# Chunk 1's inputs and head weights asked for on the SP queue, and the bias made later, in a gated low-rank kernel

## The chip, the core and the metric

One core of a Trainium2 chip. The metric is the time of the kernel on the device in microseconds (us), the median over runs. The core has TensorE (PE, matmuls, with its weight loads shown apart as PEld), VectorE (DVE), ScalarE (ACT), GpSimd (POOL) and SyncE (SP); SP and ACT each issue transfers on a queue of their own, and 16 DMA engines carry them all.

## The reference

For 2048 tokens of width 512: a linear layer, plus for each token the two best of 8 experts by logits (with 5.0 added for the expert that the sequence's id names), each expert a rank-16 update, and the input added back.

```python
x = x + L0(x, ids, W, Wr, A, B)     # x: (64, 32, 512)

def L0(x, ids, W, Wr, A, B):        # W 512x512, Wr 8x512, A 8x16x512, B 8x512x16
    base = einsum('btd,od->bto', x, W)
    logits = einsum('btd,ed->bte', x, Wr) + one_hot(ids, 8)[:, None, :] * 5.0
    topw, topi = top_k(logits, 2)
    gates = sum(one_hot(topi, 8) * softmax(topw)[..., None], axis=-2)
    h = einsum('btd,erd->bter', x, A)
    lora_out = einsum('bter,bte,eor->bto', h, gates, B)
    return base + 2.0 * lora_out
```

## The kernel before

The tokens form 16 tiles of 128. The contraction over 512 is cut into 4 chunks of 128 (k = 0 to 3). The stationary operand is a tile's x, transposed; the moving operand is the row of weights of that chunk, 648 columns: 392 *heads* columns (256 columns of W, the 128 of A and the 8 of Wr, names `heads_cols`, `heads_ps`) and 256 *base* columns (the rest of W, `base_cols`, `base_ps`).

To keep float32 accuracy, x and the weights are each split in an upper part (rounded to fp32r) and a lower part (the difference), and each product is made three times: upper by upper, upper by lower, lower by upper (n = 0, 1, 2). The parts are made on the core: `x_hi` by ACT (`chunk_upper`, L234), `x_lo` by POOL (`chunk_lower`, L213), the upper weights `w_hi` by ACT (`w_upper`, L237) but for the heads columns of chunks 0 and 1, which DVE makes (`heads_upper`, L369), and the lower weights `w_lo` by DVE (`w_lower`, L365).

Each engine runs its own program, written out by hand, and all order between engines comes from semaphores. There is no scheduler. The program starts with tiles 0 and 1 together, chunk by chunk, as the data arrives. `first_sb` holds for each chunk the x of these two tiles (256 columns), 4 columns with the ids, and the 648 weight columns. Its transfers are these: SP issues x and ids of chunk 0 (L166, 130 KB), the base weights of chunk 0 (L167, 128 KB), the base weights of chunk 1 (L168, 128 KB), and chunks 2 and 3 whole (L170, 454 KB each), then x of tile 2, b, and the groups of three tiles. ACT issues the head weights of chunk 0 (L255, 196 KB) and x, ids and head weights of chunk 1 (L256, 326 KB).

PE first runs seven matmuls on constants (L509), then one product of chunk 0 straight from float32 (L514), which needs only x and the head weights of chunk 0, and then the split products (all of them at L436). For chunk 1 it takes in this order: upper heads, upper base, the products with `x_lo`, then those with `w_lo` heads and `w_lo` base. Chunks 2 and 3 follow in nearly the same order. After that come tile 2 and a steady loop over the other tiles.

DVE starts with chunk 0 (`heads_upper(0)`, `w_lower` for heads and base), then makes the bias (L379: 5.0 where the expert's number equals the id, from `expert`, which POOL makes, and the ids in chunk 0's transfer), then chunk 1 (`heads_upper(1)` at L382, which waits for `chunk_landed[0]`, then `w_lower` for heads and base), then chunks 2 and 3, b, and from there the choice of experts. The bias is first read at L307, when PE has finished the heads of tile 0.

Of the kernel before, what the change touches and what calls it, by code (L numbers as in the profile page):

```python
# [23 lines left out]
HEADS = REST + ER + E  # L24
# [14 lines left out]
def cond_resid_program(nc: bass.Bass, first: bass.AP, xT: bass.AP, x: bass.AP,  # L39
# [11 lines left out]
    with ctx:  # L51
# [103 lines left out]
        @block.sync  # L155
        def _(sp):
            def load(dst, src, t, n, landed):
                sp.dma_start(dst[:, bass.ds(t, n), :], src[:, bass.ds(t, n), :]).then_inc(landed, 16)

            def store(t, n):  # L160
                sp.dma_start(out[:, bass.ds(t, n), :], out_sb[:, bass.ds(t, n), :]).then_inc(out_stored, 16)

            def load_xT(t, n, landed):
                load(xT_sb, xT, t - len(FIRST), n, landed)

            sp.dma_start(first_sb[:, 0, 0:FIRST_X + IDS], first[:, 0, 0:FIRST_X + IDS]).then_inc(x_landed, 16)  # L166
            sp.dma_start(w_sb[:, 0, base_cols], w[:, 0, base_cols]).then_inc(wb_landed, 16)  # L167
            sp.dma_start(w_sb[:, 1, base_cols], w[:, 1, base_cols]).then_inc(wb1_landed, 16)  # L168
            for k in range(2, KC):
                sp.dma_start(first_sb[:, k, :], first[:, k, :]).then_inc(chunk_landed[k - 1], 16)  # L170
            load_xT(2, 1, xT_third)
            sp.dma_start(b_sb[:, :], b).then_inc(b_landed, 16)

            load_xT(3, SLOTS, xT_group)
            load(x_sb, x, 0, SLOTS, x_group)
            with sp.Fori(0, GROUPS - 2) as g:
                sp.wait_ge(xT_group, 16 * g + 16)
                sp.wait_ge(x_group, 16 * g + 16)
                load_xT(SLOTS * g + 3 + SLOTS, SLOTS, xT_group)
                load(x_sb, x, SLOTS * g + SLOTS, SLOTS, x_group)  # L180
            sp.wait_ge(x_group, 16 * (GROUPS - 1))
            load(x_sb, x, GROUPED - SLOTS, SLOTS, x_group)
            load_xT(GROUPED, TILES - GROUPED, xT_last)
            load(x_sb, x, GROUPED, TILES - GROUPED, x_last)
            with sp.Fori(0, GROUPS) as g:
                sp.wait_ge(out_made, SLOTS * g + SLOTS)
                store(SLOTS * g, SLOTS)
            for t in range(GROUPED, TILES - 2):
                sp.wait_ge(out_made, t + 1)
                store(t, 1)  # L190

            for t in range(TILES - 2, TILES):
                sp.wait_ge(heads_read, t + 1)
                sp.dma_start(out[:, t, BASE:O], out_sb[:, t, BASE:O]).then_inc(out_stored, 16)
                sp.wait_ge(out_made, t + 1)
                sp.dma_start(out[:, t, 0:BASE], out_sb[:, t, 0:BASE]).then_inc(out_stored, 16)
            sp.wait_ge(out_stored, 16 * (GROUPS + TILES - 2 - GROUPED + 4))
# [33 lines left out]
        @block.scalar  # L231
        def _(act):
            def chunk_upper(k):
                nc.scalar.activation(x_hi[:, 0:2, chunks[k]], first_x[k], ACT.Copy).then_inc(chunk_hi_made, 1)  # L234

            def w_upper(k, cols):
                nc.scalar.activation(w_hi[:, k, cols], w_sb[:, k, cols], ACT.Copy).then_inc(w_hi_made, 1)  # L237

            def x_upper(t, s, landed, count):

                act.wait_ge(landed, count)
                if not (isinstance(t, int) and t < SLOTS):
                    act.wait_ge(base_done, t - SLOTS + 1)
                nc.scalar.activation(x_hi[:, s, :], xT_sb[:, t - len(FIRST), :], ACT.Copy).then_inc(x_hi_made, 1)  # L244

            def ghT_upper(t, s, src=ghT_ps):
                act.wait_ge(transposed, t + 1)
                nc.scalar.activation(ghT_hi[s][:, :], src[:, 0:P], ACT.Copy).then_inc(ghT_hi_made, 1)  # L248

            def exponential(t):  # L250
                act.wait_ge(top_made, t + 1)
                nc.scalar.activation(e2[:, :], top[:, 0:1], ACT.Exp, scale=-1.0,  # L252
                                     bias=top[:, 1:2]).then_inc(e2_made, 1)

            act.dma_start(w_sb[:, 0, heads_cols], w[:, 0, heads_cols]).then_inc(wh_landed, 16)  # L255
            act.dma_start(first_sb[:, 1, 0:FIRST_X + IDS + HEADS],  # L256
                          first[:, 1, 0:FIRST_X + IDS + HEADS]).then_inc(chunk_landed[0], 16)
            act.wait_ge(x_landed, 16)
            chunk_upper(0)
            act.wait_ge(wb_landed, 16)  # L260
            w_upper(0, base_cols)
            for k in range(1, KC):
                act.wait_ge(chunk_landed[k - 1], 16)
                chunk_upper(k)
                if k == 1:
                    act.wait_ge(wb1_landed, 16)
                    w_upper(k, base_cols)
                else:
                    w_upper(k, all_cols)
            x_upper(2, 2, xT_third, 16)  # L270
            act.wait_ge(b_landed, 16)
            nc.scalar.activation(b_hi[:, :], b_sb[:, :], ACT.Copy).then_inc(b_hi_made, 1)
            exponential(0)

            def step(t, j, landed, count):

                x_upper(t + 1, (j + 1) % SLOTS, landed, count)
                ghT_upper(t - 1, (j - 1) % SLOTS)
                exponential(t)

            exponential(1)
            ghT_upper(0, 0)
            with act.Fori(0, GROUPS - 1) as g:
                for j in range(2, 2 + SLOTS):
                    step(SLOTS * g + j, j, xT_group, 16 * g + 16)
            for t in range(GROUPED - 1, TILES - 1):
                step(t, t, xT_last, 16)
            last = TILES - 1
            act.wait_ge(x_last, 16)
            act.wait_ge(out_made, last - SLOTS + 1)  # L290
            nc.scalar.activation(base_ps[last % SLOTS][:, 0:BASE], x_sb[:, last, 0:BASE],
                                 ACT.Copy).then_inc(last_x_placed, 1)
            exponential(last)
            ghT_upper(last - 1, (last - 1) % SLOTS)
            ghT_upper(last, last % SLOTS, warm_ps)

        @block.vector
        def _(dve):
# [69 lines left out]
            def heads_upper(k):  # L368
# [5 lines left out]
            w_lower(0, heads_cols)  # L374
            dve.wait_ge(w_hi_made, 1)
            w_lower(0, base_cols)
            dve.wait_ge(expert_made, 1)
            dve.wait_ge(x_landed, 16)
            nc.vector.tensor_scalar(bias[:, :], expert[:, :], ids_sb, LANG_BIAS, ALU.is_equal,  # L379
                                    ALU.mult).then_inc(bias_made, 1)  # L380
            dve.wait_ge(chunk_landed[0], 16)
            heads_upper(1)  # L382
            dve.wait_ge(wh_hi_made, 2)
            w_lower(1, heads_cols)
            dve.wait_ge(w_hi_made, 2)
            w_lower(1, base_cols)
            for k in range(2, KC):
# [249 lines left out]
```

## Time and profile before

| | us |
|---|---|
| median of 3 runs | 79.89 |
| lowest and highest | 79.57, 80.69 |
| the profiled execution | 79.78 |
| its span | 78.0 |
| PE busy in it | 74.6 (96%) |
| PE weight loads (PEld) | 70.8 (91%) |
| DVE busy | 48.5 (62%) |
| ACT busy | 22.4 (29%) |
| POOL busy | 22.4 (29%) |

The span is what the trace covers; the time of an execution has a little more around it. A busy share is an average over the whole span. PE is busy almost throughout, so that the profile has to be read at the places where it could have been held up, above all while the first data arrives.

### The profile page before, as it was taken

What the parts mean: (1) busy time and instruction counts of PE and PEld (TensorE: products, weight loads), DVE (VectorE), ACT (ScalarE), POOL (GpSimd) and SP (SyncE); (2) the same over time, 40 slices, a digit from 0 to 9 for tenths busy, and PEclk for the clock granted to TensorE, in tenths of its full rate; (3) what the DMA queues carried; (4) which work ended last, traced back from release to release, by engine and by line L of the source; (5) the groups of instructions that cost most, each with busy time, mean ns of one, the idle gap of its engine ahead of it and who ended that gap; (6) DMA issues with size and microseconds to landing.
All of it is one profiled execution on the core that took longest, in us unless ns stands there. A gap on an engine that the chain in (4) does not pass through costs nothing.

```text
span 78.0 us, 1627 instructions
## 1 busy us (share of the span) xinstructions
PE 74.6 (96%) x502; PEld 70.8 (91%) x502; DVE 48.5 (62%) x220; ACT 22.4 (29%) x57; POOL 22.4 (29%) x26
## 2 busy tenths in 40 slices
PE   5999999999999999999999999999999999999960
PEld 2269999899999999999999999999999999999950
DVE  0097587878864828283755829283755739787750
ACT  1743941514502314140504113140404023122100
POOL 4053725064160514124060605123060606000000
PEclk9999999999999999999999999999999999999999
DMA  1999994499389389999920000350000072032143
GB/s 13 317 312 358 424 413 192 50 384 380 48 303 429 60 274 420 437 248 377 415 95 0 0 0 0 167 236 0 0 0 0 0 296 107 0 134 97 42 139 135
DMA packets 4037, 14.24 MB, mean 183 GB/s; under 512 B 448, under 2 KB 1472, under 8 KB 3776
## 3 DMA queue, kind: packets, MB, share of 16 engines
q1 hardware_dynamic: 3744, 13.65, 47.8%
q10 hardware_dynamic: 288, 0.53, 1.9%
q8 instruction: 2, 0.03, 0.2%
q14 instruction: 3, 0.02, 0.1%
HBM read 9.99 MB, written 4.19 MB: 182 GB/s over the span
## 4 chain that ended last, share of the span: by engine, by line
PE 96%; DVE 1%; issue 0%
PE heads_ps L436 43%; PE base_ps L436 28%; PE heads_ps L476 5%; PE base_ps L476 5%; PE warm_ps L509 4%; PE base_ps L480 2%; PE heads_ps L480 2%; PE ghT_ps L467 2%; PE heads_ps L514 2%; PE base_ps L460 2%; DVE out_sb L428 1%; PE warm_ps L467 0%
## 5 line engine op out<-in xcount | busy, mean ns | idle before, releaser
L209 POOL TENSOR_TENSOR x_lo<-xT_sb,x_hi 128x512 fp32r<-128x512 f32 x14 | 18.1, 1294 | 38.2 <-ACT x_hi L244 36.8
L436 PE MATMUL heads_ps<-w_hi,x_hi 128*128 128x392 f32 x63 | 22.7, 368 | 0.0
L436 PE MATMUL heads_ps<-w_lo,x_hi 128*128 128x392 f32 x63 | 20.9, 340 | 0.0
L436 PE MATMUL heads_ps<-w_hi,x_lo 128*128 128x392 f32 x63 | 20.8, 342 | 0.0
L436 PE MATMUL base_ps<-w_hi,x_lo 128*128 128x256 f32 x60 | 16.6, 283 | 0.0
L436 PE MATMUL base_ps<-w_hi,x_hi 128*128 128x256 f32 x60 | 16.6, 288 | 0.0
L436 PE MATMUL base_ps<-w_lo,x_hi 128*128 128x256 f32 x60 | 16.3, 280 | 0.0
L301 DVE TENSOR_TENSOR ghT_lo<-ghT_ps,ghT_hi 128x128 fp32r<-128x128 f32 x15 | 4.4, 291 | 14.8 <-ACT ghT_hi L248 14.7
L248 ACT ACTIVATE ghT_hi<-ghT_ps 128x128 fp32r<-128x128 f32 x15 | 4.1, 275 | 29.5 <-PE ghT_ps L467 29.5
L436 PEld LDWEIGHTS heads_ps<-w_hi,x_hi 128*128 128x128 f32 x63 | 11.8, 190 | 0.8 <-issue 0.3
L436 PEld LDWEIGHTS base_ps<-w_hi,x_hi 128*128 128x128 f32 x60 | 11.5, 193 | 0.4 <-ACT w_hi L237 0.3
L436 PEld LDWEIGHTS heads_ps<-w_lo,x_hi 128*128 128x128 f32 x63 | 11.7, 189 | 0.0
L436 PEld LDWEIGHTS heads_ps<-w_hi,x_lo 128*128 128x128 f32 x63 | 11.6, 188 | 0.0
L436 PEld LDWEIGHTS base_ps<-w_hi,x_lo 128*128 128x128 f32 x60 | 11.4, 192 | 0.0
L436 PEld LDWEIGHTS base_ps<-w_lo,x_hi 128*128 128x128 f32 x60 | 11.3, 189 | 0.0
L252 ACT ACTIVATE e<-top 128x1 f32<-128x1 f32 x16 | 4.7, 296 | 15.2 <-DVE top L312 15.2
L244 ACT ACTIVATE x_hi<-xT_sb 128x512 fp32r (+1 forms) x14 | 8.7, 621 | 0.4 <-issue 0.4
L346 DVE TENSOR_TENSOR out_sb<-heads_ps,x_sb 128x256 f32 (+1 forms) x16 | 6.7, 419 | 1.1 <-PE heads_ps L480 1.1
L336 DVE SCALAR_TENSOR_TENSOR gh<-heads_ps,rden,gate 128x128 f32<-128x128 f32 x16 | 5.6, 351 | 1.7
L351 DVE TENSOR_TENSOR out_sb<-base_ps,x_sb 128x256 f32 (+1 forms) x15 | 6.2, 415 | 0.0
L365 DVE TENSOR_TENSOR w_lo<-first_sb,w_hi 128x392 fp32r<-128x392 f32 (+1 forms) x8 | 4.5, 596 | 1.5 <-ACT w_hi L237 1.4
L213 POOL TENSOR_TENSOR x_lo<-first_sb,x_hi 128x256 fp32r<-128x256 f32 (+1 forms) x5 | 3.5, 705 | 5.1 <-ACT x_hi L234 5.1
(53 smaller groups left out, 99.9 us busy)
## 6 DMA issues: line engine op xcount, KB each, us to landing
x_sb<-in_x SPq DMA_DIRECT2D x4, 768.0 KB, 5.5
out<-out_sb SPq DMA_DIRECT2D x4, 768.0 KB, 4.3
xT_sb<-in_xT SPq DMA_DIRECT2D x3, 768.0 KB, 4.2
xT_sb<-in_xT SPq DMA_DIRECT2D x1, 1024.0 KB, 6.4
x_sb<-in_x SPq DMA_DIRECT2D x1, 1024.0 KB, 9.4
first_sb<-in_first SPq DMA_DIRECT2D x2, 454.0 KB, 5.6
out<-out_sb SPq DMA_DIRECT2D x2, 256.0 KB, 2.1
out<-out_sb SPq DMA_DIRECT2D x4, 128.0 KB, 1.8
```

Source lines behind the costliest of these rows:

```text
L209: nc.gpsimd.tensor_tensor(x_lo[:, s, :], xT_sb[:, t - len(FIRST), :], x_hi[:, s, :].bitcast(FP32), ALU.subtract).then_inc(x_lo_made, 1)
L213: nc.gpsimd.tensor_tensor(x_lo[:, tiles, chunks[k]], first_x[k][:, tiles, :], x_hi[:, tiles, chunks[k]].bitcast(FP32), ALU.subtract).then_ ...
L244: nc.scalar.activation(x_hi[:, s, :], xT_sb[:, t - len(FIRST), :], ACT.Copy).then_inc(x_hi_made, 1)
L248: nc.scalar.activation(ghT_hi[s][:, :], src[:, 0:P], ACT.Copy).then_inc(ghT_hi_made, 1)
L252: nc.scalar.activation(e2[:, :], top[:, 0:1], ACT.Exp, scale=-1.0, bias=top[:, 1:2]).then_inc(e2_made, 1)
L301: nc.vector.tensor_tensor(ghT_lo[s][:, :], src[:, 0:P], ghT_hi[s][:, :].bitcast(FP32), ALU.subtract).then_inc(ghT_lo_made, 1)
L336: nc.vector.scalar_tensor_tensor(gh[s][:, :].rearrange("p (e r) -> p e r", r=R), heads_ps[s][:, REST:REST + ER].rearrange("p (e r) -> p e ...
L346: nc.vector.tensor_tensor(out_sb[:, t, BASE:O], heads_ps[s][:, 0:REST], x_sb[:, t, BASE:O], ALU.add).then_inc(heads_read, 1)
L351: nc.vector.tensor_tensor(out_sb[:, t, 0:BASE], base_ps[s][:, 0:BASE], x_sb[:, t, 0:BASE], ALU.add).then_inc(out_made, 1)
L365: nc.vector.tensor_tensor(w_lo[:, k, cols], w_sb[:, k, cols], w_hi[:, k, cols].bitcast(FP32), ALU.subtract).then_inc(w_lo_made, 1)
L436: return nc.tensor.matmul(dst, xs[:, s, chunks[k]], ws[:, k, cols], start=(k == 0 and n == 0), stop=(k == KC - 1 and n == last_n))
L476: nc.tensor.matmul(dst, ghT_hi[s][:, :], bs[:, cols], start=False, stop=False, skip_group_check=True)
```

## The change

The transfer of chunk 1 (x, ids and head weights, 326 KB) is no longer issued by ACT behind the head weights of chunk 0. SP issues it, third in its queue: behind the base weights of chunk 0 and ahead of the base weights of chunk 1. On DVE the upper and lower head weights of chunk 1 are made before the bias, and the lower base weights of chunk 1 after it. Nothing else differs, and PE's program is the same row for row.

```diff
--- before.py
+++ after.py
@@ -165,6 +165,8 @@
 
             sp.dma_start(first_sb[:, 0, 0:FIRST_X + IDS], first[:, 0, 0:FIRST_X + IDS]).then_inc(x_landed, 16)
             sp.dma_start(w_sb[:, 0, base_cols], w[:, 0, base_cols]).then_inc(wb_landed, 16)
+            sp.dma_start(first_sb[:, 1, 0:FIRST_X + IDS + HEADS],
+                         first[:, 1, 0:FIRST_X + IDS + HEADS]).then_inc(chunk_landed[0], 16)
             sp.dma_start(w_sb[:, 1, base_cols], w[:, 1, base_cols]).then_inc(wb1_landed, 16)
             for k in range(2, KC):
                 sp.dma_start(first_sb[:, k, :], first[:, k, :]).then_inc(chunk_landed[k - 1], 16)
@@ -253,8 +255,6 @@
                                      bias=top[:, 1:2]).then_inc(e2_made, 1)
 
             act.dma_start(w_sb[:, 0, heads_cols], w[:, 0, heads_cols]).then_inc(wh_landed, 16)
-            act.dma_start(first_sb[:, 1, 0:FIRST_X + IDS + HEADS],
-                          first[:, 1, 0:FIRST_X + IDS + HEADS]).then_inc(chunk_landed[0], 16)
             act.wait_ge(x_landed, 16)
             chunk_upper(0)
             act.wait_ge(wb_landed, 16)
@@ -374,14 +374,14 @@
             w_lower(0, heads_cols)
             dve.wait_ge(w_hi_made, 1)
             w_lower(0, base_cols)
+            dve.wait_ge(chunk_landed[0], 16)
+            heads_upper(1)
+            dve.wait_ge(wh_hi_made, 2)
+            w_lower(1, heads_cols)
             dve.wait_ge(expert_made, 1)
             dve.wait_ge(x_landed, 16)
             nc.vector.tensor_scalar(bias[:, :], expert[:, :], ids_sb, LANG_BIAS, ALU.is_equal,
                                     ALU.mult).then_inc(bias_made, 1)
-            dve.wait_ge(chunk_landed[0], 16)
-            heads_upper(1)
-            dve.wait_ge(wh_hi_made, 2)
-            w_lower(1, heads_cols)
             dve.wait_ge(w_hi_made, 2)
             w_lower(1, base_cols)
             for k in range(2, KC):
```

SP's program at its start, before the change (`first_sb` is the tile that holds the first chunks; 128x260 is x and ids of chunk 0, 128x256 base weights, 128x908 a whole chunk):

```order
L166 DMA first_sb<-in_first 128x260
L167 DMA first_sb<-in_first 128x256
L168 DMA first_sb<-in_first 128x256
L170 DMA first_sb<-in_first 128x908 x2
L158 DMA xT_sb<-in_xT 128x512
L172 DMA b_sb<-in_b 128x512
```

and after it:

```order
L166 DMA first_sb<-in_first 128x260
L167 DMA first_sb<-in_first 128x256
L168 DMA first_sb<-in_first 128x652
L170 DMA first_sb<-in_first 128x256
L172 DMA first_sb<-in_first 128x908 x2
L158 DMA xT_sb<-in_xT 128x512
L174 DMA b_sb<-in_b 128x512
```

The row of 128x652 (chunk 1's x, ids and head weights) is new, and every row below it stands one place further back.

DVE's program, the piece that differs, with the semaphores that each row waits for (the rows of w_lo are lower weights, 128x392 heads and 128x256 base; the CAST of w_hi makes chunk 1's upper head weights):

```order
 L365 TENSOR_TENSOR w_lo<-first_sb,w_hi 128x392 [waits wh_hi_made]
 L365 TENSOR_TENSOR w_lo<-first_sb,w_hi 128x256 [waits w_hi_made]
-L379 TENSOR_SCALAR bias<-expert,first_sb 128x8 [waits x_landed,expert_made]
 L369 CAST w_hi<-first_sb 128x392 [waits chunk_landed1]
 L365 TENSOR_TENSOR w_lo<-first_sb,w_hi 128x392 [waits wh_hi_made]
+L383 TENSOR_SCALAR bias<-expert,first_sb 128x8 [waits x_landed,expert_made]
 L365 TENSOR_TENSOR w_lo<-first_sb,w_hi 128x256 [waits w_hi_made]
 L365 TENSOR_TENSOR w_lo<-first_sb,w_hi 128x392 [waits w_hi_made]
```

The bias has moved down by two rows, past chunk 1's upper and lower head weights.

## Rows read from the trace of the kernel before

**Rows 1.** The page: its span, and the chain that ended last by engine.
```profile
span 78.0 us, 1627 instructions
...
PE 96%; DVE 1%; issue 0%
```

**Rows 2.** Chain in order of time: start us, us, what.
```profile
0.78 3.14 PE warm_ps L509 x7
3.93 1.58 PE heads_ps L514 x2
...
5.83 0.72 PE base_ps L436 x4
6.55 0.35 PE heads_ps L436 x2
```

**Rows 3.** Timeline, DVE: start us, us, engine line, operation, tiles, [idle before <-releaser].
```profile
3.75 0.37 DVE L369 CAST w_hi<-first_sb 128x392 fp32r<-128x392 f32 x1 [3.75 <-DMA first_sb<-in_first]
4.15 1.45 DVE L365 TENSOR_TENSOR w_lo<-first_sb,w_hi 128x392 fp32r<-128x392 f32 x2
5.52 0.49 DVE L379 TENSOR_SCALAR bias<-expert,first_sb 128x8 f32<-128x8 int32 x1
5.92 0.35 DVE L369 CAST w_hi<-first_sb 128x392 fp32r<-128x392 f32 x1
6.31 1.04 DVE L365 TENSOR_TENSOR w_lo<-first_sb,w_hi 128x392 fp32r<-128x392 f32 x2
```

**Rows 4.** Busy us of PE, PEld, DVE, ACT, POOL; PEclk, DMA share, GB/s.
```profile
3.86:6.26 2.40, 2.40 (x7) 1.77 (x7) 2.37 (x5) 1.24 (x4) 1.46 (x3) 1.00 1.00 321
6.26:11.96 5.70, 5.70 (x40) 5.70 (x39) 3.79 (x9) 3.15 (x6) 2.52 (x4) 1.00 1.03 405
```

**Rows 5.** Timeline, PE's weight loads (PEld).
```profile
5.30 0.66 PEld L436 LDWEIGHTS base_ps<-w_hi,x_hi 128*128 128x128 f32 x2 [0.32 <-ACT w_hi L237]
...
6.87 0.30 PEld L436 LDWEIGHTS heads_ps<-w_hi,x_hi 128*128 128x128 f32 x2
...
8.36 0.37 PEld L436 LDWEIGHTS base_ps<-w_lo,x_hi 128*128 128x128 f32 x2
8.66 0.30 PEld L436 LDWEIGHTS heads_ps<-w_hi,x_hi 128*128 128x128 f32 x2
```

**Rows 6.** Timeline, ACT.
```profile
3.54 0.42 ACT L234 ACTIVATE x_hi<-first_sb 128x256 fp32r<-128x256 f32 x1 [0.58 <-DMA first_sb<-in_first]
4.72 0.42 ACT L237 ACTIVATE w_hi<-first_sb 128x256 fp32r<-128x256 f32 x1 [0.77 <-DMA first_sb<-in_first]
...
7.42 0.42 ACT L234 ACTIVATE x_hi<-first_sb 128x256 fp32r<-128x256 f32 x1 [1.25 <-DMA first_sb<-in_first]
7.74 0.73 ACT L237 ACTIVATE w_hi<-first_sb 128x648 fp32r<-128x648 f32 x1
```

**Rows 7.** Timeline, issues; then issue to landing, L256 and the first of L170.
```profile
1.19 0.46 ACTq L256 DMA_DIRECT2D first_sb<-in_first  x1
1.66 0.42 SPq L168 DMA_DIRECT2D first_sb<-in_first  x1
...
2.13 0.91 SPq L170 DMA_DIRECT2D first_sb<-in_first  x2
...
DMA to landing us min/median/max: 3.7/3.7/3.7
...
DMA to landing us min/median/max: 5.3/5.3/5.3
```

**Rows 8.** Timeline, POOL.
```profile
5.53 1.06 POOL L213 TENSOR_TENSOR x_lo<-first_sb,x_hi 128x128 fp32r<-128x128 f32 x2 [0.76 <-ACT x_hi L234]
```

**Rows 9.** Line L365, subtractions one by one: ns min/median/max, start us.
```profile
L365 DVE TENSOR_TENSOR w_lo<-first_sb,w_hi x1: 1035/1035/1035, 4.2 to 4.2; 128x392 fp32r<-128x392 f32 x1
...
L365 DVE TENSOR_TENSOR w_lo<-first_sb,w_hi x1: 703/703/703, 6.3 to 6.3; 128x392 fp32r<-128x392 f32 x1
...
L365 DVE TENSOR_TENSOR w_lo<-first_sb,w_hi x1: 566/566/566, 8.5 to 8.5; 128x392 fp32r<-128x392 f32 x1
```

## The prediction

> **What bounds the kernel now.** I read the page first: the chain of work that ended last is 96% TensorE, in a span of 78.0 us, of which 1% is VectorE and none is a transfer [rows 1]. The question is therefore whether TensorE (PE) ever waits for what the change moves, and all of that lies in the first 9 us. The chain in order of time shows PE there as one unbroken run of matmuls: seven warm-up matmuls from 0.78, the first real pair (L514) from 3.93, the matmul of line L436 behind it, four base products for 0.72 us from 5.83, two heads products for 0.35 from 6.55, and so on [rows 2]. No wait stands between them. What begins at 3.93 is what the reader is to follow: the start is set by the landing of chunk 0's head weights, at 3.75 [rows 3], and no transfer that the change moves.
>
> The pace has a step. The warm-up takes 3.14 us for 7 matmuls of 512 columns, 0.45 each, which is 1.14 columns a ns, so the 1.2 GHz level; behind 6.55 two matmuls of 392 columns take 0.35, 2.2 columns a ns, the 2.4 GHz level [rows 2]. By the four base products (two at 0.213 and two at 0.117 would be 0.66; 0.72 is shown) the step lies at about 6.3 us. PE had been busy since 0.78 when it came. The granted clock reads 1.00 on both sides of it [rows 4], so this page doesn't show the step as a grant; I read it from the matmul pace alone. This matters for the slack: PE reaches chunk 1 late because its first 5.5 us are slow.
>
> Then I listed, for each product, when PE takes its operand (the weight-load rows) [rows 5] and when the operand was ready (producer's start plus duration).
> - Chunk 0, upper base weights: ScalarE (ACT) 4.72 + 0.42 = 5.14 [rows 6]; load at 5.30 [rows 5]. Slack 0.16, and the load could not come sooner, as the matmul in front has only then taken its own weights.
> - Chunk 1, upper head weights: VectorE (DVE) 5.92 + 0.35 = 6.27 [rows 3]; load 6.87 [rows 5]. Slack 0.60.
> - Chunk 1, lower head weights: the two subtractions that begin at 6.31 take 1.04 to 7.35 [rows 3]. The heads part takes 703 ns of them [rows 9] and is ready at 7.01. The base part's load is at 8.36 [rows 5]: slack 1.0. The heads part's pair of loads, 0.30 long like the pair at 8.66 [rows 5], stands right ahead, at 8.06: slack 1.05.
> - Chunk 2, upper weights: ACT 7.74 + 0.73 = 8.47 [rows 6]; load 8.66 [rows 5]. **Slack 0.19, the smallest of all behind the start**, and its producer waited 1.25 us for a transfer until 7.42 [rows 6].
>
> **The change part by part.** (1) *The transfer of chunk 1 leaves ACT's queue.* ACT issued it at 1.19 and it landed 3.7 us later [rows 7], at 4.9. ACT's next work, at 3.54, waits for a landing and not for the issue [rows 6]; what ACT saves, 0.46 us of issue, lies in an idle stretch: 0. (2) *Chunk 0's base weights no longer compete with it.* They now share the engines only with the 130 and 196 KB in front, so they land before 4.72, by at most the time of chunk 1's bytes moved till then. What follows is ACT's copy, whose slack was 0.16 already and whose user can't start sooner. Gain 0. DVE's second subtraction doesn't gain either: it follows the first, which began at 4.15; both take 1.45 [rows 3].
>
> (3) *Chunk 1 is issued third on the SP queue*, at 1.66 in place of 1.19, where chunk 1's base weights were [rows 7]. What has to land by its end is the same 780 KB as before (130 + 196 + 128 + 326), and the 16 DMA engines are full from 3.86 on (share 1.00, then 1.03) [rows 4], so from below it lands at 4.9, unchanged. From above: chunk 2 lands at 7.42 [rows 6], 0.47 later by point (5), and 582 KB (128 + 454) go between the two, 1.44 us at 405 GB/s [rows 4]; that puts chunk 1 at 6.45. DVE would copy till 6.81 and the load at 6.87 [rows 5] would find it; POOL's two subtractions, 1.06 long [rows 8] behind ACT's copy of x of 0.42, would end at 7.93, some 0.2 behind the loads of their products, which stand a little ahead of 8.06. So 0.2 is the price at that end. I take a landing near 5.0, with the full engines, and no cost. Gain and loss 0.
>
> (4) *DVE copies chunk 1's heads before the bias.* The bias stood at 5.52 and the copy began 0.40 later, at 5.92 [rows 3]. Chunk 1 had landed at 4.9, so the copy can begin at 5.52 and ends at 5.87 in place of 6.27. The subtraction begins at 5.91 in place of 6.31. It then lies wholly beside GpSimd's (POOL) two subtractions, which start at 5.53 and take 1.06 [rows 8]. Such a subtraction took 566 ns with little of POOL beside it and 1035 ns beside POOL [rows 9]; so it ends between 6.48 and 6.95, against 7.01 now. The 0.40 gained is mostly given back there, all of it under the slack of 1.05. The bias takes its 0.4 after it, and the base part of chunk 1 comes last of all: 6.95 + 0.40 + 0.41 = 7.76 at the latest, against the load at 8.36 [rows 5]: slack 0.6, no cost. Behind the bias on DVE nothing else waits, and its reader comes after PE's first finished tile, several us later: 0. If PE's cover for (4) were gone, the price would be at most the 0.40 that the base part comes later.
>
> The Trainium skill, SBUF — State Buffer (shared GpSimd/Vector port), says that a VectorE operation with two SBUF inputs and a GpSimd operation hold one port pair exclusively, the later one blocked until the other is done. By that rule (4) could push POOL's second half to about 7.0, and the sum would still be the same. The trace agrees, with 1035 ns beside POOL [rows 9].
>
> (5) *Every later issue of SP moves back by one step*, 0.47 us (1.66 to 2.13) [rows 7]: chunk 1's base weights, chunks 2 and 3, tile 2, b, the groups. Chunk 2 is the one that counts. Now it lands 5.3 us after its issue at 2.13 [rows 7], at 7.43. It needs 1362 KB through the engines in either version, and they are full; so from below its landing doesn't move (0). From above it follows its issue, 0.47 later; then ACT's copy ends at 8.94 and PE stalls 0.47 − 0.19 = 0.28. Its first bytes are due about 6.3 (7.42 less 454 KB at 405 GB/s), and it is issued at 2.60 even then, 3.7 us ahead; that is nearer to "doesn't move". I take 0, and keep 0.28. Chunk 3 and the rest stand behind more slack.
>
> Sum: 0 + 0 + 0 + 0 + 0 on the profiled execution's 79.78 us (78.0 span and 1.8 around it), which is 0.1 under the median of 79.89. I forecast **79.8**.
>
> The Trainium skill, DMA: Bandwidth & Descriptors, "Issuing engines are not separate DMA queues", says that issuing from several engines saves only the sequencer's issue time. That speaks against this change, which gives up just that: by it alone the sum would be +0.28, 80.1. The full engines in this trace say it costs nothing.
>
> **The rivals.**
> *A, hidden (the forecast), 0.72.* Slacks as above. 79.8, own range 79.5 to 80.2.
> *B, slower: chunk 2 lands late, 0.12.* For it: the smallest slack of the list and one more issue in front. Against: the full DMA engines. It decides from a landing after 7.61; full price 0.28: 80.1.
> *C, faster: the start comes earlier, 0.08.* The DMA engines no longer hold chunk 1's packets while the first two transfers finish. x lands at 3.54 [rows 6], the head weights at 3.75 [rows 3]; at best they land together, PE starts 0.2 sooner and everything moves: 79.6. Against: both were issued first on their queues, before chunk 1. Part of the gain would be eaten at chunk 2, whose slack is 0.19.
> *D, the pace step moves, 0.08.* Each us by which the step from 1.2 to 2.4 GHz comes later costs 0.5 us; each us by which it comes earlier gives 0.5, but only until chunk 2's copy at 8.47 stops PE, thus 0.19 in all: a floor of 79.6, which is what the fastest run shows (79.57). The slowest, 80.69, would be a step 1.8 us later. The change gives no cause for it, yet the median of a few runs can carry it: 79.6 to 80.7.
> The Trainium skill, TensorE: Matmul & The Clock Gate (Part 1), says that the point at which the full clock comes varies from run to run for one and the same kernel. No row of a single execution can show that; the spread of the three runs fits it.
>
> **How the numbers follow.** A and B and C together hold 79.5 to 80.2; D stretches the upper end, where it has no floor: a step 1.4 us later gives 80.5. Below, C on top of the floor gives 79.4. Range 79.4 to 80.5. Two per cent is 1.6 us, about what a measurement of this kernel can tell from no change. No case reaches it alone: the gain is capped by the 0.2 of C, the loss of B is 0.28, and D would need a step 3 us later. Same 0.95, slower 0.03 (D with B), faster 0.02.
>
> **What would show it.** Right: the first load at 3.8 as before; DVE's copy of chunk 1 at about 5.5, the subtraction behind it slow (0.9 to 1.0) because POOL runs beside it, the bias at about 7, the lower base part ending before 7.8; ACT's copy of chunk 0's base weights before 4.72; chunk 2's wait on ACT ending at 7.4; PE's loads of chunks 1 and 2 following without a gap. Wrong in (5): that wait ends past 7.6 and PE idles before chunk 2's first load. Wrong in (3): DVE idles past 6.5 for chunk 1. Wrong in C's favour: the first load before 3.7. If the matmuls keep the slow pace past 6.3 us, D is at work and the span must be read with that taken off.

## The result, and the profile after

| | before | after |
|---|---|---|
| median of 22 runs, us | 79.84 | 80.11 |
| ratio, 95% interval | | 1.0038 (1.0021 to 1.0056) |
| the profiled execution, us | 79.78 | 80.11 |
| its span, us | 78.0 | 78.2 |

The change makes the kernel 0.3 us slower: far below 2%, but clear of zero (0.17 to 0.45 us). The forecast was no change at all, 79.8. The ratios, here and below, leave out executions more than 1.5% above the fastest of the same kernel; two such runs are far out, 148.5 us (before) and 257.1 us (the change).

The page of the changed kernel, its span and the chain that ended last:

```profile
span 78.2 us, 1627 instructions
...
PE 96%; DVE 1%; issue 0%
```

TensorE bounds it as before [rows 1]. Its chain in order of time (start us, us, what):

```profile
0.78 3.15 PE warm_ps L509 x7
...
3.95 1.64 PE heads_ps L514 x2
...
5.92 0.82 PE base_ps L436 x4
6.74 0.36 PE heads_ps L436 x2
```

Against [rows 2] the start is 0.02 later, the first pair takes 1.64 in place of 1.58, and the four base products take 0.82 in place of 0.72: the slow pace lasts a little longer in this execution. From 6.55 against 6.74 the lead is 0.19 us, and it does not grow behind that. So in this pair of executions the 0.2 us of span arose ahead of chunk 1, and none of it is a wait for chunk 1; what the change costs on average has to come from more executions. Now PE's weight loads:

```profile
3.92 0.50 PEld L514 LDWEIGHTS heads_ps<-first_sb 128*128 128x128 f32 x2 [0.90 <-DMA first_sb<-in_first]
...
7.06 0.30 PEld L436 LDWEIGHTS heads_ps<-w_hi,x_hi 128*128 128x128 f32 x2
...
7.77 0.19 PEld L436 LDWEIGHTS base_ps<-w_hi,x_lo 128*128 128x128 f32 x1
7.98 0.19 PEld L436 LDWEIGHTS heads_ps<-w_hi,x_lo 128*128 128x128 f32 x1
...
8.86 0.30 PEld L436 LDWEIGHTS heads_ps<-w_hi,x_hi 128*128 128x128 f32 x2
```

They follow without a gap, 0.19 to 0.20 later than in [rows 5] (7.06 against 6.87, 8.86 against 8.66). The load at 7.98 is the one to remember: it takes tile 1's lower x of chunk 1. The engines that make the operands, ACT first, then DVE, in the timeline:

```profile
4.09 0.42 ACT L239 ACTIVATE w_hi<-first_sb 128x256 fp32r<-128x256 f32 x1
5.96 0.42 ACT L236 ACTIVATE x_hi<-first_sb 128x256 fp32r<-128x256 f32 x1 [1.45 <-DMA first_sb<-in_first]
...
7.40 0.42 ACT L236 ACTIVATE x_hi<-first_sb 128x256 fp32r<-128x256 f32 x1 [0.71 <-DMA first_sb<-in_first]
7.72 0.73 ACT L239 ACTIVATE w_hi<-first_sb 128x648 fp32r<-128x648 f32 x1
...
5.96 0.37 DVE L369 CAST w_hi<-first_sb 128x392 fp32r<-128x392 f32 x1 [0.34 <-DMA first_sb<-in_first]
6.36 0.57 DVE L365 TENSOR_TENSOR w_lo<-first_sb,w_hi 128x392 fp32r<-128x392 f32 x1
6.85 0.43 DVE L383 TENSOR_SCALAR bias<-expert,first_sb 128x8 f32<-128x8 int32 x1
```

and POOL's two halves of chunk 1's lower x, the first alone and then both (line L215: ns shortest/median/longest, start us):

```profile
L215 POOL TENSOR_TENSOR x_lo<-first_sb,x_hi x1: 795/795/795, 6.5 to 6.5; 128x128 fp32r<-128x128 f32 x1
...
L215 POOL TENSOR_TENSOR x_lo<-first_sb,x_hi x2: 711/753/795, 6.5 to 7.2; 128x128 fp32r<-128x128 f32 x2
```

Four things are to be seen. Chunk 0's base copy starts at 4.09 in place of 4.72 [rows 6], and nobody is the better for it. **Chunk 1 lands at 5.96, in place of 4.9**: both ACT and DVE wait for it. Chunk 2 lands at 7.40, in place of 7.42: the extra issue has not moved it. And POOL's halves take 795 and 711 ns where they took 1.06 us for both [rows 8]; they end near 7.9, right at the load at 7.98. Before the change they ended at 6.6 [rows 8] and the load that takes the second half stood at 7.76:

```profile
7.76 0.19 PEld L436 LDWEIGHTS heads_ps<-w_hi,x_lo 128*128 128x128 f32 x1
```

A cover of over a microsecond is used up.

The landing can be read from the issue too, at 1.66, line L168 of the changed kernel:

```profile
DMA to landing us min/median/max: 4.3/4.3/4.3
```

How much had moved by then (the columns of [rows 4]; first the changed kernel, then the one before):

```profile
0.00:5.96 5.96, 5.16 (x12) 2.30 (x13) 1.74 (x3) 2.12 (x3) 1.55 (x8) 1.00 0.67 216
```

```profile
0.00:4.90 4.90, 4.12 (x10) 1.62 (x10) 1.11 (x2) 1.88 (x3) 1.54 (x8) 1.00 0.65 201
```

By the landing of chunk 1, 985 KB had moved before the change (4.90 us at 201 GB/s) and 1287 KB after it, while the four transfers up to and with chunk 1 hold about 800 in both. The DMA engines were as full as I had said (share 0.98 from 3.86 to 6.26, against 1.00), but with bytes that stood behind chunk 1.

The packet records of the two traces show how a landing gets late. Chunk 1 is moved in 128 rows. Before the change half of them had ended at 3.98, 112 at 4.30 and the last at 4.52; with the change half had ended at 4.20, 112 at 4.89, and the last only at 5.53. A transfer has landed when its last row has, and a few rows came very late.

The trace of before had a warning that I did not read. The place in question, third on SP's queue, was taken there by chunk 1's base weights, only 128 KB, issued at 1.66 (L168). ACT waited for them until 5.75:

```profile
5.75 0.42 ACT L237 ACTIVATE w_hi<-first_sb 128x256 fp32r<-128x256 f32 x1 [0.30 <-DMA first_sb<-in_first]
```

With the change chunk 1 stands in that place and lands at 5.96, and its base weights, now fourth, land at 6.24 in place of 5.72.

### The profile page after: what moved, and what is told of

Same layout as the page of the kernel before. It is cut to its first block, busy times and chain, and to the rows that moved or that the text cites. A ratio compares the mean times of both kernels' runs of the same rounds, so it can differ in the third digit from the quotient of the medians.

```text
span 78.2 us, 1627 instructions
## 1 busy us (share of the span) xinstructions
PE 74.8 (96%) x502; PEld 70.9 (91%) x502; DVE 48.2 (62%) x220; ACT 22.4 (29%) x57; POOL 22.7 (29%) x26
## 4 chain that ended last, share of the span: by engine, by line
PE 96%; DVE 1%; issue 0%
PE heads_ps L436 43%; PE base_ps L436 28%; PE heads_ps L476 5%; PE base_ps L476 5%; PE warm_ps L509 4%; PE base_ps L480 2%; PE heads_ps L480 2%; PE ghT_ps L467 2%; PE heads_ps L514 2%; PE base_ps L460 2%; DVE out_sb L428 1%; PE warm_ps L467 0%
## 5 line engine op out<-in xcount | busy, mean ns | idle before, releaser
L215 POOL TENSOR_TENSOR x_lo<-first_sb,x_hi 128x256 fp32r<-128x256 f32 (+1 forms) x5 | 3.8, 765 | 4.8 <-ACT x_hi L236 4.8
L365 DVE TENSOR_TENSOR w_lo<-first_sb,w_hi 128x392 fp32r<-128x392 f32 (+1 forms) x8 | 4.3, 565 | 1.3 <-ACT w_hi L239 1.2
```

Of the source, the lines that this page charges most:

```text
L215: nc.gpsimd.tensor_tensor(x_lo[:, tiles, chunks[k]], first_x[k][:, tiles, :], x_hi[:, tiles, chunks[k]].bitcast(FP32), ALU.subtract).then_ ...
L365: nc.vector.tensor_tensor(w_lo[:, k, cols], w_sb[:, k, cols], w_hi[:, k, cols].bitcast(FP32), ALU.subtract).then_inc(w_lo_made, 1)
```

## The experiments

All comparisons are with the kernel before on the same chip. "Time minus span" is the mean over the timed executions of a kernel of the execution's time less its span in the same execution; its standard error is about 0.01 us. ACT's length is the number of instructions of ACT in the trace against the kernel before, which has 108.

| kernel | ratio (95% interval) | chunk 1 lands | time − span | ACT's length |
|---|---|---|---|---|
| before (35 executions) | 1 | 4.9 | 1.81 | 0 |
| the change | 1.0038 (1.0021 to 1.0056) | 5.96 | 1.93 | −1 |
| e4 the change again | 1.0025 (1.0001 to 1.0050) | 5.0 | 1.92 | −1 |
| e12 the change, third | 1.0025 (0.9998 to 1.0053) | 5.9 | 1.93 | −1 |
| e8 before again | 1.0000 (0.9970 to 1.0029) | 5.0 | 1.80 | 0 |
| e1 transfer only | 1.0010 (0.9981 to 1.0040) | 6.1 | 1.91 | −1 |
| e2 order only | 1.0011 (0.9989 to 1.0033) | 5.1 | 1.79 | 0 |
| e5 one more issue | 0.9999 (0.9980 to 1.0019) | 5.1 | 1.82 | 0 |
| e6 chunk 1 fourth | 1.0091 (1.0065 to 1.0117) | 6.25 | 1.93 | −1 |
| e3 base 1 on ACT | 1.0019 (0.9998 to 1.0041) | 6.35 | 1.81 | 0 |
| e7 chunk 1 second | 1.0031 (1.0006 to 1.0056) | 4.9 | 1.80 | 0 |
| e9 x first | 1.0027 (1.0004 to 1.0050) | x 5.0 | 1.94 | −1 |
| e10 before, 9 warm-ups | 0.9988 (0.9948 to 1.0027) | 4.9 | 1.80 | 0 |
| e11 change, 9 warm-ups | 1.0026 (1.0004 to 1.0048) | 5.9 | 1.93 | −1 |
| f13 change, ACT 2 transfers | 1.0034 (1.0013 to 1.0055) | 5.7 | 1.82 | 0 |
| f14 before, ACT 3 transfers | 1.0222 (1.0162 to 1.0283) | 8.45 | 1.79 | +1 |
| f15 change, late ACT transfer | 1.0015 (0.9987 to 1.0042) | 6.15 | 1.81 | +1 |
| f16 change, ACT none | 1.0101 (1.0074 to 1.0128) | 6.4 | 1.80 | −2 |
| g1 change, ACT longer | 1.0014 (0.9983 to 1.0044) | 5.25 | 1.81 | 0 |
| g2 ACT none, longer | 1.0131 (1.0090 to 1.0172) | 6.45 | 1.93 | −1 |

**Which part of the change, and how sure.** e1 puts the bias back:

```diff
+            dve.wait_ge(expert_made, 1)
+            dve.wait_ge(x_landed, 16)
+            nc.vector.tensor_scalar(bias[:, :], expert[:, :], ids_sb, LANG_BIAS, ALU.is_equal,
+                                    ALU.mult).then_inc(bias_made, 1)
             dve.wait_ge(chunk_landed[0], 16)
             heads_upper(1)
             dve.wait_ge(wh_hi_made, 2)
             w_lower(1, heads_cols)
-            dve.wait_ge(expert_made, 1)
-            dve.wait_ge(x_landed, 16)
-            nc.vector.tensor_scalar(bias[:, :], expert[:, :], ids_sb, LANG_BIAS, ALU.is_equal,
-                                    ALU.mult).then_inc(bias_made, 1)
```

> The changed kernel with the bias back in its old place on VectorE: only the transfer of chunk 1 is moved to SP's queue. Theory T (the transfer costs it all): as slow as the change, +0.2 to +0.45 us over before; chunk 1 lands at 5.7 to 6.1 in place of 4.9. Rival V (VectorE's order costs it): within 0.1 us of before. In the trace of the change chunk 1 landed at 5.96, the first matmul started 0.09 later and the matmul pace doubled 0.2 to 0.3 us later than in the trace of before.

e2 is the kernel before with only these rows moved as in the change:

> The kernel before with VectorE's order of the change alone: chunk 1's heads ahead of the bias, the transfer still on ACT's queue. Theory T: within 0.1 us of before, with the copy of chunk 1 at about 5.5 and nothing on TensorE that moves. Rival V: +0.2 to +0.45.

e4 and e12 are the changed kernel unchanged, e8 is the kernel before:

> The changed kernel once more, on the same chip as the others, for a second trace of it. If the later start (first weight load at 3.92 against 3.83) and the later change of pace are its own, they are seen again: start 3.88 to 3.96, time +0.2 to +0.45. If they belong to one execution, the start goes back to 3.83 or so while the time stays +0.3: then the cause lies behind the start.

> The changed kernel a third time, for a third trace and for the spread of its runs. Theory L: +0.15 to +0.4 over before; chunk 1 lands near 6.0 rather than 5.0, and the load of the second tile's product with the lower x comes right behind GpSimd's second half.

> The kernel before once more as a kernel of its own: a second trace of it, and a measure of what the comparison gives for no change. All theories: within 0.15 us of before; chunk 1 lands at 4.8 to 5.2 again (theory L), with the first weight load anywhere from 3.83 to 4.1 and the change of pace anywhere from 4.9 to 6.5.

The ratios of e1 and e2 lie between no change and the change and settle nothing alone; e1's 0.08 us is below the 0.2 to 0.45 that theory T had set. What else they show does tell the two apart: with the transfer moved (e1) chunk 1 lands at 6.1 and time minus span is 1.91, with the order alone (e2) they are 5.1 and 1.79. e8 shows what no change looks like, 1.0000, and that the later start is no property of the change: e8, which is the kernel before, has its first weight load at 3.96. The three comparisons of the change give 0.20 to 0.30 us (e12's interval just holds 1).

The landing is not always late. In e4 it came at 5.0 and in e12 at 5.9; this is ACT's row in e4, then in e12:

```profile
5.03 0.42 ACT L236 ACTIVATE x_hi<-first_sb 128x256 fp32r<-128x256 f32 x1 [0.42 <-DMA first_sb<-in_first]
```

```profile
5.86 0.42 ACT L236 ACTIVATE x_hi<-first_sb 128x256 fp32r<-128x256 f32 x1 [1.26 <-DMA first_sb<-in_first]
```

Over one trace each, chunk 1 in third place on SP's queue landed between 5.7 and 6.35 in seven of nine kernels (the change, e1, e3, e11, e12, f13, f15) and at 5.0 and 5.25 in two (e4, g1). In second place on ACT's queue it landed between 4.9 and 5.1 in all five (before, e2, e5, e8, e10).

**What the late chunk costs.** e5 leaves chunk 1 on ACT's queue and delays everything behind by an issue:

```diff
-            sp.dma_start(w_sb[:, 1, base_cols], w[:, 1, base_cols]).then_inc(wb1_landed, 16)
+            for at in range(HEADS, WIDTH, BASE // 2):
+                sp.dma_start(w_sb[:, 1, at:at + BASE // 2], w[:, 1, at:at + BASE // 2]).then_inc(wb1_landed, 16)
...
-                    act.wait_ge(wb1_landed, 16)
+                    act.wait_ge(wb1_landed, 32)
```

> The kernel before, with chunk 1's base weights asked for in two halves on SP (two issues of 64 KB, the same bytes), so that chunk 2 and all behind it are issued 0.47 us later as in the change, while chunk 1's x and heads stay on ACT's queue. Theory S (the later issue of chunk 2 costs): chunk 2 lands 0.2 to 0.47 later and the time is +0.2 to +0.3 over before. Theory L (the late landing of chunk 1 costs, chunk 2's landing does not depend on its issue): within 0.12 of before.

e6 swaps chunk 1's two transfers on SP:

```diff
+            sp.dma_start(w_sb[:, 1, base_cols], w[:, 1, base_cols]).then_inc(wb1_landed, 16)
             sp.dma_start(first_sb[:, 1, 0:FIRST_X + IDS + HEADS],
                          first[:, 1, 0:FIRST_X + IDS + HEADS]).then_inc(chunk_landed[0], 16)
-            sp.dma_start(w_sb[:, 1, base_cols], w[:, 1, base_cols]).then_inc(wb1_landed, 16)
```

> The change with a larger dose: chunk 1's x and heads are fourth on SP's queue, behind chunk 1's base weights. Theory L: chunk 1 lands 0.3 to 0.5 later again (6.3 to 6.6), POOL's lower parts of it end past 7.9, TensorE waits for them in most executions: +0.5 to +0.8 over before. Theory S: as the change, +0.25, since the number of issues ahead of chunk 2 is the same.

The pair decides between lateness of chunk 1 and the number of issues: the extra issue alone gives 0.9999, the larger dose 1.0091, 0.73 us, within the 0.5 to 0.8 expected. In e6 PE's loads wait for POOL, twice:

```profile
7.62 0.19 PEld L436 LDWEIGHTS heads_ps<-w_hi,x_lo 128*128 128x128 f32 x1 [0.20 <-POOL x_lo L215]
...
8.29 0.19 PEld L436 LDWEIGHTS heads_ps<-w_hi,x_lo 128*128 128x128 f32 x1 [0.37 <-POOL x_lo L215]
```

In the mean e6's span is 0.6 longer than that of before on its chip. The same waits stand in kernels with chunk 1 third: in e12 and f15, for instance (one line of each, in this order),

```profile
7.88 0.19 PEld L436 LDWEIGHTS heads_ps<-w_hi,x_lo 128*128 128x128 f32 x1 [0.25 <-POOL x_lo L215]
```

```profile
8.18 0.19 PEld L440 LDWEIGHTS heads_ps<-w_hi,x_lo 128*128 128x128 f32 x1 [0.38 <-POOL x_lo L217]
```

and also 0.17 in e1 and 0.38 in f13. None of the five kernels with chunk 1 on ACT's queue in the old place has one. POOL is not the only one waited for: PE's first load of chunk 1 waits for ACT's copy of its x, 0.29 in e3 and 0.43 in f15, and in e12 its load of the upper base weights waits 0.23 for ACT, as those weights, fourth on SP's queue, landed only at 6.6.

e3 moves chunk 1's base weights from SP's to ACT's queue; e7 moves chunk 0's base weights there, so that chunk 1 is second on SP. The row that each adds on ACT, behind the head weights (e3's, then e7's):

```diff
+            act.dma_start(w_sb[:, 1, base_cols], w[:, 1, base_cols]).then_inc(wb1_landed, 16)
...
+            act.dma_start(w_sb[:, 0, base_cols], w[:, 0, base_cols]).then_inc(wb_landed, 16)
```

> The change, with chunk 1's base weights (128 KB) issued by ACT behind the head weights of chunk 0, so that both queues have work in the first 5 us; chunk 1's x and heads stay on SP. Theory Q (a slower delivery because only one queue is filled): chunk 1 lands before 5.4, and the time comes back by half or more, to within 0.15 us of before. Rival P (it is the place third on SP's queue that makes chunk 1 late): chunk 1 at 5.8 or later and the time as in the change, +0.3.

> The change with chunk 1's x and heads second on SP's queue and chunk 0's base weights second on ACT's in exchange: chunk 2 is issued at the same place as before the change. Theory L: chunk 1 lands by 5.2 and the time is that of before, within 0.15, or 0.1 less; chunk 0's base weights land near 4.4. If the time stays at +0.25 with chunk 1 early, theory L is wrong.

In e3 chunk 1 came later still, at 6.35, so a second filled queue does not help it: the place third on SP is what makes it late (rival P), though the time, 1.0019, lies between both expectations. In e7 chunk 1 landed 3.7 us after its issue at 1.19, exactly as on ACT's queue: in this one trace it is the place that counts (and the issue 0.47 us earlier that goes with it), not whose queue. But the time stayed at 1.0031, which by its own terms speaks against theory L. The trace offers a reason, found afterwards, ACT's row and then PE's:

```profile
5.14 0.42 ACT L238 ACTIVATE w_hi<-first_sb 128x256 fp32r<-128x256 f32 x1 [1.10 <-DMA first_sb<-in_first]
```

```profile
5.61 0.50 PEld L436 LDWEIGHTS base_ps<-w_hi,x_hi 128*128 128x128 f32 x2 [0.56 <-ACT w_hi L238]
```

Now chunk 0's base weights are late (5.1, where I expected 4.4), PE waits for them, and ACT, which takes its work in order, copies chunk 1's x only at 5.46. So e7 may have moved the cost one step forward in place of removing it; that this is the whole of 1.0031 is argued, not shown.

e9 lets chunk 1's x go ahead of its weights:

```diff
-            sp.dma_start(first_sb[:, 1, 0:FIRST_X + IDS + HEADS],
-                         first[:, 1, 0:FIRST_X + IDS + HEADS]).then_inc(chunk_landed[0], 16)
+            sp.dma_start(first_sb[:, 1, 0:FIRST_X + IDS], first[:, 1, 0:FIRST_X + IDS]).then_inc(chunk_landed[0], 16)
+            sp.dma_start(w_sb[:, 1, heads_cols], w[:, 1, heads_cols]).then_inc(wh1_landed, 16)
...
-            dve.wait_ge(chunk_landed[0], 16)
+            dve.wait_ge(wh1_landed, 16)
```

> The change with its new transfer in two: chunk 1's x (130 KB) third on SP, chunk 1's head weights (196 KB) fourth, each with its own semaphore; the same bytes in the same order, one more issue. Theory L' (what TensorE waits for is GpSimd's lower part of chunk 1's x, which in the trace of the change ends at 7.9 since x lands at 5.96): x lands at 5.0 to 5.4, both lower halves are made by 7.2, and the time comes back to within 0.12 us of before. Rival W (the late head weights are what costs): still +0.25, as these land at 6.0 or later.

x landed at 5.0 and POOL was done by 6.5, as expected, and PE's loads of chunks 1 and 2 had no gap. The time did not come back: 1.0027, 0.22 us. But 0.13 of that lies outside the span (time minus span is 1.94 here; what that hangs on comes below), where an earlier x could change nothing; about 0.1 stays in the span. The trace shows a wait that I had not looked at, 8 us further on, here in e9 and then in e5:

```profile
14.38 0.30 PE L468 MATMUL ghT_ps<-ident,gh 128*128 128x128 f32 x1 [0.41 <-DVE gh L337]
```

```profile
13.98 0.30 PE L468 MATMUL ghT_ps<-ident,gh 128*128 128x128 f32 x1 [0.34 <-DVE gh L337]
```

The transpose of tile 0's gated values waits for DVE, in whose program the lower weights of chunk 3 and of b come first. ACT took chunk 3 at 8.97 in e9, where two issues more stand ahead of it than before the change, against 8.55 in before. In e5 it took it at 8.57, hardly later, but PE was there sooner. So a second path, through chunk 3 and DVE, ends about as late as PE's own work, and a gain at chunk 1 can be lost there. That it was lost there in e9 is not shown: e5 has nearly the same wait and no loss of time (0.9999).

e10 and e11 are the kernels before and after with

```diff
-WARM_UP = 7
+WARM_UP = 9
```

> The kernel before with 9 warm-up matmuls in place of 7: the first product can start only at about 4.8. It takes 0.85 us more on TensorE at the slow pace, part of it given back since less real work is left for the slow pace: +0.35 to +0.7 over before. It is here for its difference to the next kernel.

> The changed kernel with 9 warm-up matmuls: TensorE reaches chunk 1 later, so its late landing is covered. Theory L: no slower than the kernel before with 9 (difference 0, at most 0.1). If the cost of the change came from elsewhere than a wait for chunk 1 (bandwidth lost, a slower steady state), the difference stays at +0.25.

The pair decides nothing. By the ratios of the table the change costs 0.30 us with nine warm-ups too (1.0026 against 0.9988), where theory L had allowed 0.1; by the medians of all runs it is faster (80.15 against 80.51). The difference is six of e10's twelve runs, from 80.75 us up, which the ratio leaves out; its runs lie between 79.4 and 81.3, in two groups. In e11's trace PE's loads have no wait for POOL, with chunk 1 at 5.9, so the cover was there, but the time does not show that it helped.

**What lies outside the span.** The spans alone do not hold the loss: leaving out executions above 80.6 us, the mean span is 78.06 (102 executions) before and 78.14 (44) with the change, 0.08 more with a standard error of 0.04. Over all eight kernels with chunk 1 third and seven warm-ups (the change, e1, e3, e4, e12, f13, f15, g1) it is 78.18 (104), 0.11 more than in 129 executions of before, with a standard error of 0.03. Time minus span, however, is 1.81 and 1.93. That is 0.12 us in every comparison, ten times its error. The next six kernels ask what it hangs on. f13 halves chunk 0's head weights on ACT's queue in the change, f14 does the same in the kernel before:

```diff
-            act.dma_start(w_sb[:, 0, heads_cols], w[:, 0, heads_cols]).then_inc(wh_landed, 16)
+            for at in range(0, HEADS, HEADS // 2):
+                act.dma_start(w_sb[:, 0, at:at + HEADS // 2], w[:, 0, at:at + HEADS // 2]).then_inc(wh_landed, 16)
...
-            dve.wait_ge(wh_landed, 16)
+            dve.wait_ge(wh_landed, 32)
...
-            pe.wait_ge(wh_landed, 16)
+            pe.wait_ge(wh_landed, 32)
```

> The change, with chunk 0's head weights asked for by ACT in two halves (98 KB each), so that ACT issues two transfers as before the change. Over all timed executions so far, time minus span is 1.81 in kernels in which ACT issues two transfers and 1.91 to 1.94 in those in which it issues one. Theory O (a cost outside the span that hangs on how many transfers ACT issues): time minus span goes back to 1.80 to 1.83. Rival R (it hangs on chunk 1's bytes going over SP's queue): it stays at 1.91 to 1.94.

> The kernel before with the same halving: ACT issues three transfers. Theory O in its simplest form, a threshold at two: time minus span stays at 1.81. If it falls with each transfer: 1.70. Rival R: 1.81. The span grows by 0 to 0.3, as chunk 1 is issued 0.47 later.

f15 adds a transfer that nothing uses near the end of ACT's program, and a wait for it as the last row, f16 issues chunk 0's head weights on SP:

```diff
+            act.dma_start(spare[:, :], w[:, 0, base_cols]).then_inc(spare_landed, 16)
             act.wait_ge(x_last, 16)
...
+            act.wait_ge(spare_landed, 16)
```

> The change with a second transfer on ACT's queue that nothing uses (128 KB into a spare tile), issued shortly before the last tile. Theory O: time minus span 1.80 to 1.83, wherever the second transfer stands in the program. If it has to be among the first instructions of ACT: 1.91 to 1.94.

> The change with chunk 0's head weights second on SP's queue as well: ACT issues nothing. Theory O, by a count: time minus span above 1.94, or below 1.81 if it is the mere use of ACT's queue that costs. The first weight load is 0.2 to 0.5 later than 3.9, the span +0.1 to +0.5.

With two transfers on ACT the 0.12 us are gone (f13 1.82, f15 1.81), wherever the second stands; with three too (f14 1.79, over six executions), and with none as well (f16 1.80). "Exactly one" is an odd law. What also differs is the length of ACT's program (the wait that f15 adds makes it two instructions longer than the change), so g1 is the change and g2 is f16 with one instruction more at the end of it:

```diff
+        spare = sb("spare", [P, E])
...
             ghT_upper(last, last % SLOTS, warm_ps)
+            nc.scalar.activation(spare[:, :], x_sb[:, last, 0:E], ACT.Copy)
```

> The change (one transfer issued by ACT) with one more instruction at the end of ACT's program, a copy of 8 columns that nothing uses. ACT's program is then as long as before the change. Theory C (exactly one transfer issued by ACT is what costs): time minus span stays at 1.91 to 1.94. Rival N (the length of ACT's program is what counts, as no kernel so far tells the two apart): 1.79 to 1.83. The span as in the change.

> The kernel in which ACT issues no transfer, with the same copy at the end: ACT's program is now as long as that of the change. Theory C: time minus span 1.80, as without the copy. Rival N: 1.91 to 1.94.

g1: one transfer, 1.81. g2: none, 1.93. It goes with the length (rival N). In all 20 rows of the table, 1.91 to 1.94 stands where ACT's program is one instruction shorter than before (107 in the trace), and 1.79 to 1.82 where it is two shorter, equal or one longer. SP's program does not sort them: it is one instruction longer than before in e5 (1.82) as in the change (1.93). The change removed one instruction from ACT, and with that come 0.12 us outside the span. Why just this length costs is open. The ratios of f13, f15 and g1 (1.0034, 1.0015, 1.0014) have intervals too wide to show 0.15% by themselves.

The spans of f14 and f16 grew by more than expected. In f16 everything is on SP, and chunk 1, fourth there, landed at 6.4; PE waited 0.80 for ACT's copy of its x. f14's loss, 2.2%, with chunk 1 third on ACT's queue, is not explained: its only trace is of an execution of 83.4 us (chunk 1 at 8.45, PE waits 2.03 for it), and the four of 81.3 to 82.3 us on which the ratio rests have none.

## Why the prediction was wrong

*What bounds the kernel* held: PE's chain, 96%, and an end that is fixed in the start-up. So did the reading of a change of pace near 6.3 us and its spread. L514's two passes took 1.58 in the trace of before, 1.65 in e8 (the same kernel), 1.64 in the change and 1.27 in e4 (the same change); so mechanism D is at work in every comparison, as noise. It also made the 0.2 us between the two profiled spans: that these show the cost of the change at all is luck.

*(1) ACT's issue: 0.* **Failed, by 0.12 us.** Nothing in the span was lost by it, as predicted; but the sum stood on 78.0 of span "and 1.8 around it", taken over without a reason, and the 1.8 became 1.93. It goes with ACT's program being one instruction shorter (g1 and g2); by what mechanism is open.

*(2) Chunk 0's base weights earlier: 0.* Right: copy at 4.09 in place of 4.72, no user sooner.

*(3) Chunk 1 lands near 5.0, cost 0.* **Failed.** It landed at 5.96, and in seven traces of nine 0.8 to 1.4 us later than before. The step that was wrong is the inference from full DMA engines: that 780 KB ahead of a landing take as long in either order. Engines that are full may carry what stands behind; 1287 KB had moved by then, and the last few of chunk 1's 128 rows came a microsecond late. My upper end, 6.45 with a price of 0.2 at POOL's halves, was the right place and nearly the right size: PE's loads idle there for 0.17 to 0.59 us in e1, e12, f13 and f15 (nothing in the changed kernel's own first two traces), and in the mean over executions the span grew by 0.08. I had put the value near the wrong end of a range that I had. That end had a second place that I missed: ACT's copy of x would end at 6.45 + 0.42 = 6.87, just when PE's first load of chunk 1 stands, and my list of slacks had neither this copy nor chunk 1's upper base weights.

*(4) The order on DVE: 0.* Right for DVE (e2: 1.0011, with 0 in the interval; bias at 6.85, no reader waits). But the late chunk put DVE's subtraction and POOL's halves side by side again, and POOL's took 1.51 (795 + 711 ns) in place of the 1.06 that I had carried over into (3). By the Trainium skill, SBUF — State Buffer (Who interferes with whom), the pair of ports that a DVE operation with two SBUF inputs shares with POOL is exclusive, and whoever comes second fully blocks. The trace shows operations that get longer, which would fit a wait inside them.

*(5) The later issues: 0.* Right for the issue by itself: with chunk 1 left in its place one more issue gives 0.9999 (e5), and in the change chunk 2 landed at 7.40. The Trainium skill says in DMA: Bandwidth & Descriptors (Issuing engines are not separate DMA queues) that a second issuing engine saves only the issue's own time. The prediction made +0.28 of that, and no run shows such a price: what the second queue had saved was a place, and with it about a microsecond of chunk 1's landing. e5's trace also shows a wait at 14 us by way of chunk 3 that the list of slacks had left out.

One rival is not tested apart. Over the traces chunk 2 landed between 6.9 and 7.8 (mean 7.5) in the nine kernels with chunk 1 third, and between 6.7 and 7.6 (mean 7.2) in the five with it on ACT's queue. In e12 and g1, and also in e2, PE's first load of chunk 2 comes 0.11 behind the end of ACT's copy and 0.32 to 0.50 behind the load before it, where the pace is about 0.18. So part of what the span lost may have been lost at chunk 2.

*Rival B* had nearly the right sum, 0.28, but that is luck: in the changed kernel's trace chunk 2 did not move, and 0.12 us of the sum lie outside the span. *Rival C* did not appear: the first load was at 3.92, and between 3.83 and 4.00 in the other four traces of the two kernels.

Together: 0.12 outside the span (shown, with its cause open) and 0.08 in it, with a standard error of 0.04, give 0.20 us. That the second part comes from waits for chunk 1 is supported by the dose (e6) and by the waits in the traces, but not settled: the kernels that brought chunk 1 or its x early again (e7, e9) did not bring the span back, and nine warm-ups did not close the difference. Two of the three comparisons gave 0.20, the first 0.30 with 0.20 inside its interval.

## What to carry to other kernels

A DMA engine share of 1.0 says that work is conserved, not that your transfer keeps its place: take the landing of a moved transfer from one that stood in that place (here 5.72, in the trace of before), and if there is none, cost its users at the late end. List the slack of each user over every engine behind the landing, the last and slowest one above all (here POOL), and look past the start-up for a second path that ends as late. For effects of a few tenths of a microsecond, compare time minus span as well: its standard error was 0.01 us over 12 executions, and it can move by itself.

## What the runs showed of the hardware

- The time outside the span goes with the length of ACT's program: in the 20 rows of the table it was 1.91 to 1.94 us at one instruction fewer than before, and 1.79 to 1.82 at two fewer, at the same number and at one more, whatever the instruction was (a transfer, or a copy of 8 columns). The cause is open.
- A transfer of 326 KB took 3.7 us from issue to landing in second place on SP's queue (e7), 3.7 to 3.9 in second place on ACT's (five traces), and 4.0 to 4.7 in seven of nine traces in third place on SP's. The lateness was in its last rows: 112 of 128 had ended at 4.89 and the last at 5.53 (the change), against 4.30 and 4.52 (before).
- The granted clock reads 1.00 in every stretch of the traces of before and the change, yet the matmuls run at the pace of the 1.2 GHz level at first, and in traces of one kernel the change of pace came at different times, after PE had been busy since 0.78: L514's pair and the four base products behind it took 1.64 and 0.82 us in the change, 1.27 and 0.48 in e4. From these I estimate the change of pace at about 6.7 and 4.9 us.
- POOL's subtraction of 128 columns took 457 ns with DVE's bias beside it (before), and 795 and 711 ns with DVE's subtractions of weights beside it (the change).
